# A vision tower on one core: the first group's batches in a new hand-written order, with sums in SBUF and the weights scaled on GpSimd

## The reference

```
h   = leaky(bn1(conv(x, stem_w, 4x4, stride 4)))        # 96 channels, 24 x 24
off = conv(h, off_w, 4x4, stride 4)                      # 32 channels, 6 x 6: a (y, x) offset for each of 16 taps
h   = leaky(bn2(deform_conv(h, off, dcn_w)))             # each tap samples h at a shifted point, from 4 corners
                                                         # 192 channels, 36 tokens an image
h   = h + attention(layernorm(h))                        # linear attention with random features, 12 heads
h   = h + experts(layernorm(h))                          # 3 experts of 192 x 768, top-1 gate per image
```

## Time and profile before

| what | value |
|---|---|
| median of 3 runs | 449.45 us (449.16 to 450.73) |
| the profiled execution's own time | 449.24 us |
| its span | 447.4 us |
| TensorE (PE) busy | 386.6 us, 86% |
| VectorE (DVE) busy | 287.8 us, 64% |
| ScalarE (ACT) busy | 223.4 us, 50% |
| GpSimd (POOL) busy | 163.0 us, 36% |
| chain that ended last | PE 65%, ACT 16%, DVE 13% |
| DMA | 54.18 MB, mean 121 GB/s |

### The profile page before, as it was taken

How to read it: one execution, slowest core, us unless ns; L and a number is a source line. 1 busy time by engine, 2 the same in 40 slices (tenths; PEclk the granted TensorE clock), 3 DMA queues, 4 the chain that set the end, 5 groups by cost and what they waited for, 6 DMA issues and landing times.

```text
span 447.4 us, 8176 instructions
## 1 busy us (share of the span) xinstructions
PE 386.6 (86%) x2856; PEld 279.6 (62%) x2856; DVE 287.8 (64%) x1108; ACT 223.4 (50%) x529; POOL 163.0 (36%) x168
## 2 busy tenths in 40 slices
PE   7986686878899797998988979788997979899997
PEld 3665254655678354876775768478575847767575
DVE  3842465745656677796666988765698876566222
ACT  2565545555536767544544475245448524542610
POOL 4116886700207676330067645107665300000000
PEclk9685567969699959999999999999999999999999
DMA  6578576843899953324855543104544200000000
GB/s 149 145 199 249 159 168 191 224 130 81 252 258 279 315 160 92 104 71 113 206 142 131 134 110 89 54 2 122 144 128 122 72 1 2 0 1 19 2 1 21
DMA packets 58480, 54.18 MB, mean 121 GB/s; under 512 B 42314, under 2 KB 50791, under 8 KB 58439
## 3 DMA queue, kind: packets, MB, share of 16 engines
q0 software_dynamic: 9216, 28.32, 22.5%
q1 hardware_dynamic: 48584, 25.28, 21.5%
q10 hardware_dynamic: 639, 0.05, 0.1%
HBM read 38.52 MB, written 15.11 MB: 120 GB/s over the span
## 4 chain that ended last, share of the span: by engine, by line
PE 65%; ACT 16%; DVE 13%; issue 4%; DMA 1%; SPq 1%; POOL 0%; ACTq 0%; DVEq 0%; POOLq 0%
PE bank L1065 10%; PE bank L1037 7%; PE bank L774 6%; PE bank L666 5%; PE bank L1044 5%; PE bank L689 4%; PE bank L703 4%; PE bank L971 4%; ACT bank L1248 3%; DVE bank L1557 2%; ACT hid L1400 2%; DVE o L1650 2%; PE bank L935 2%; PE bank L642 2%; DVE acc L1557 2%
## 5 line engine op out<-in xcount | busy, mean ns | idle before, releaser
L598 POOL DMA_INDIRECT ring<-cells,cell x144 | 150.0, 1041 | 167.3 <-DVE mv L1617 67.1
L1400 ACT ACTIVATE hid<-bank,b_up 128x288 f32<-128x288 f32 x72 | 32.0, 498 | 63.6 <-PE bank L1044 63.5
L1557 DVE SCALAR_TENSOR_TENSOR bank<-ring,corner,bank 128x96 f32<-128x96 f32 x224 | 52.9, 311 | 8.0 <-ACT bank L1248 7.9
L1065 PE MATMUL bank<-w_down,hid 128*128 128x192 f32 x288 | 52.1, 332 | 0.0
L1037 PE MATMUL bank<-xfT,w_up 128*128 128x288 f32 x144 | 44.8, 433 | 5.5 <-ACT hid L1400 5.3
L1065 PEld LDWEIGHTS bank<-w_down,hid 128*128 128x128 f32 x288 | 46.2, 190 | 4.6 <-issue 4.4
L774 PE MATMUL bank<-w_dcn,shared 128*128 128x192 f32 x192 | 42.6, 362 | 6.1 <-ACT shared L1257 6.1
L774 PEld LDWEIGHTS bank<-w_dcn,shared 128*128 128x128 f32 x192 | 33.6, 205 | 13.7 <-ACT shared L1257 9.8
L1037 PEld LDWEIGHTS bank<-xfT,w_up 128*128 128x128 f32 x144 | 25.0, 193 | 14.9 <-ACT hid L1400 7.8
L1505 DVE SCALAR_TENSOR_TENSOR h<-h 96x768 f32<-96x768 f32 x18 | 17.5, 994 | 25.1 <-ACT h L1236 23.7
L1248 ACT ACTIVATE bank<-ring,corner 128x96 f32<-128x96 f32 x112 | 31.4, 335 | 0.2 <-DMA ring<-cells,cell 0.2
(11 more groups left out here) (203 smaller groups left out, 648.0 us busy)
## 6 DMA issues: line engine op xcount, KB each, us to landing
cells<-ring SPq DMA_DIRECT2D x12, 864.0 KB, 8.7
xs<-in_x_dram SPq DMA_DIRECT2D x28, 108.0 KB
ring<-cells,cell POOLq DMA_INDIRECT x144, 3.1
cells<-w_up SPq DMA_DIRECT2D x2, 864.0 KB, 9.4
cells<-w_down SPq DMA_DIRECT2D x2, 864.0 KB, 7.5
w_down<-in_L_ffn_W_dram SPq DMA_DIRECT2D x3, 576.0 KB
hid<-in_L_tok_dcn_w_dram SPq DMA_DIRECT2D x1, 1152.0 KB, 7.6
w_up<-in_L_ffn_W_dram SPq DMA_DIRECT2D x3, 384.0 KB
```

Of the source, the lines that this page charges most:

```text
L598: pool.indirect_dma_start(ring[:, ring_slot(k), j, :], None, cells[g][0:HALF_CELLS, :] if k < EARLY else cells[g], bass.IndirectOffsetOnAx ...
L1065: mm = pe.matmul(down_out(e, t), hid[:, e % 2, f, t0:t0 + n], w_down[:, e, f, :], start=(f == 0), stop=(f == FCH - 1))
L1400: act.activation(hid[:, e % 2, f, :], up_bank(g, n)[:, 0:TOK], ACT.Gelu, bias=b_up[:, n:n + 1]).then_inc(gelu_done, 1)
L1557: ins = dve.scalar_tensor_tensor(acc[:, k % 3, :, j, :] if c == 3 else part_sum, ring[:, ring_slot(k), j, C1 * c:C1 * (c + 1)].rearrange(" ...
```

## The change

All of it lies in the front of the kernel, up to channels(0).

- **TensorE.** Ahead of the step only row units 0 to 5 of group 0 remain. Both offset halves of group 0 follow, then turn_unit(6), offsets_by_token(0) and product_unit(6), and only then row units 6 to 11, mixed with the transposes of the weights and the stem units 7 and 8. From there one written list of calls holds the nine batches, the stem units 9 to 17, the rows of group 1 (the first six ahead of dcn_turn(0, 0)), and row units 0 to 9 of group 2. Units 10 and 11 and group 2's offset halves stand behind fold_tokens(0). Row units alternate between two banks from group 1 on, and the weights use banks 0 to 2, so that the stem's transposes no longer wait for row copies.
- **ScalarE** and **VectorE** have such lists too. Row copies are shared out: VectorE takes the six odd ones of group 0, 1 to 6 of group 1 and 1 of group 2. It also takes three of the six copies of w_dcn. scale_dcn leaves ScalarE.
- **GpSimd** scales the weights, in 24 operations of 96 x 128, between rearrange_rows(1, 0) and rearrange_rows(1, 1).
- **Sums.** All of group 0's running sums are in SBUF, three deep: the first corner of batch k waits for the transpose of batch k - 3.
- **Homes.** Group 2's rows are copied into h, whose group 1 contents are done with by then, and no longer into the ring. So group 1's gathers don't wait for their store. The stem of group 3, which writes h, waits for that store instead of the offsets.
- **Loads.** Images (2,1) are loaded right behind (2,0). ld_ffn becomes ld_up and ld_down; up() waits for ld_up, the first down() and VectorE, at the step's end, for ld_down.

The diff's core (the written lists shortened):

```diff
-        def running(k):
-            if k < IN_SBUF:
+        def running(g, k):
+            if g == 0 or k < IN_SBUF:
...
-        FRONT_TURNS = {0: 9, 1: 10, 2: 11, 4: 12, 5: 13, 6: 14, 7: 15, 8: 16}
-        FRONT_ROWS = ((), (0,), (1, 2), (4, 5), (6,), (7, 8), (9,), (10, 11), ())
...
+        ROWS_ON_DVE = (range(1, 12, 2), (1, 2, 3, 4, 5, 6), (1,), ())
...
         def row_home(g, s):
+            if g == 2:
+                return h[:, s, :, :]
             return ht_first[s] if g == 1 else ht[:, s, :, :]
...
             load_images(2, 0)
+            load_images(2, 1)
             sp.wait_ge(gathered[ring_slot(2)], slot_done(0, 2))
...
+            def scale_dcn(i):
+                m, q = i // QUADS, i % QUADS
+                src = dcn_nat[:, m, :].rearrange("o (i c j q) -> o q i j c", i=CHUNKS, c=32, j=BATCH)[:, q, :, :, :]
+                for c in range(CHUNKS):
+                    ins = pool.tensor_scalar(dcn_perm[:, m, q, 128 * c:128 * c + 128].rearrange("o (j c) -> o j c", j=BATCH),
+                                             src[:, c], bn_scale[:, 1 + m:2 + m], None, ALU.mult)
+                ins.then_inc(dcn_scaled, 1)
 
...
-            for s in range(2):
-                rearrange_rows(1, s)
+            rearrange_rows(1, 0)
+            pool.wait_ge(ld_dcn, 16)
+            pool.wait_ge(bn_ready, 1)
+            for i in range(2 * QUADS):
+                scale_dcn(i)
+            rearrange_rows(1, 1)
...
+                offset_half(0, 0)
+                offset_half(0, 1)
                 turn_unit(6)
-                for n in (7, 8):
-                    turn_unit(n)
-                    product_unit(n - 1)
+                pe.wait_ge(ld_small, 16 * 6)
+                offsets_by_token(0)
+                product_unit(6)
+                row_unit(0, 6)
+                row_unit(0, 7)
+                row_unit(0, 8)
+                turn_unit(7)
+                row_unit(0, 9)
+                dcn_weights(0)
+                row_unit(0, 10)
+                dcn_weights(1)
+                row_unit(0, 11)
+                dcn_weights(2)
+                dcn_weights(3)
+                natural()
+                turn_unit(8)
...
+                row_unit(1, 5)
+                turn_unit(12)
+                dcn_turn(0, 0)
+                row_unit(1, 6)
+                row_unit(1, 7)
+                dcn_bias_rows()
...
+                dcn_products(0, 7)
+                row_unit(2, 7)
+                dcn_turn(0, 8)
+                row_unit(2, 8)
+                dcn_products(0, 8)
+                row_unit(2, 9)
                 fold_tokens(0)
-                product_unit(17)
+                row_unit(2, 10)
+                row_unit(2, 11)
+                offset_half(2, 0)
+                offset_half(2, 1)
...
+                if g == 1:
+                    stem_rows(3)
                 if g < 2:
-                    stem_rows(g + 2)
-                    pe.wait_ge(ht_even, 6 * (g + 3))
-                    pe.wait_ge(ht_odd, 6 * (g + 3))
+                    for done, count in last_rows(g + 2, 11):
+                        pe.wait_ge(done, count)
                 channels(g, xn, xn_ready, t2_mm, ROWTILES)
...
-                    pe.wait_ge(ld_ffn, 16 * 13)
+                    pe.wait_ge(ld_up, 16 * 9)
...
-                    act.wait_ge(off_mm, 2 * (g - 2) + (s + 1))
+                    act.wait_ge(h_stored[s], 32 * g)
...
-                if k >= IN_SBUF + 2:
+                if g == 0 and k >= 3:
+                    act.wait_ge(samp_mm, k - 2)
+                elif later(g) and k >= IN_SBUF + 2:
                     act.wait_ge(combined, BATCH * (BATCHES * g + k - 1))
-                elif k >= IN_SBUF:
...
+                dcn_weights(0)
+                row_copy(0, 10)
+                stem_turned(7)
+                dcn_weights(2)
+                stem_turned(8)
                 act.wait_ge(idx_ready, 2)
                 first_corners(0, 0)
-                for k in range(BATCHES):
-                    if k + 1 < BATCHES:
-                        first_corners(0, k + 1)
-                    if k in FRONT_SCALED:
-                        stem_scaled(FRONT_SCALED[k])
...
+                part_copy(0)
+                sample_points(0)
+                row_copy(0, 7)
+                row_copy(0, 9)
+                sample_corners(0)
+                row_copy(0, 11)
+                dcn_weights(1)
+                natural()
+                dcn_weights(3)
+                leaky(1, 0, 0, 1)
+                combine(0, 0, 1)
+                leaky(1, 0, 1, 2)
+                dcn_weights(5)
+                row_copy(1, 1)
...
+                combine(0, 7, 8)
+                leaky(2, 1, 1, 2)
+                combine(0, 8, 9)
+                dcn_tokens(0, range(FULL))
+                leaky(2, 1, 2, 3)
+                sample_corners(1)
+                dcn_tokens(0, (FULL,))
...
```

More of the change, by code:

```diff
@@ new lines, in dcn_first @@
+                turn_unit(14)
+                dcn_products(0, 1)
+                row_unit(1, 9)
+                row_unit(1, 10)
+                offsets_by_token(1)
+                dcn_turn(0, 3)
+                turn_unit(15)
+                row_unit(1, 11)
+                dcn_products(0, 2)
+                product_unit(14)
+                dcn_turn(0, 4)
+                turn_unit(16)
+                row_unit(2, 0)
+                row_unit(2, 1)
+                product_unit(15)
+                turn_unit(17)
@@ L1330, in combine_first @@
-                act.wait_ge(dcn_mm, BATCHES)
-                act.activation(xn[:, FULL, :], ps[2][:, 0:C2], ACT.Copy).then_inc(parts_evac, 1)
+                stem_scaled(7)
+                dcn_weights(4)
+                stem_turned(9)
+                stem_scaled(8)
+                row_copy(1, 0)
+                stem_turned(10)
+                stem_scaled(9)
+                first_corners(0, 1)
+                dcn_bias()
+                stem_scaled(10, 0, 1)
+                stem_turned(11)
@@ L1428, in _ @@
             stem_bn(0, 1)
[L1429 to L1438 removed]
+            for u in (0, 2, 4):
+                row_copy(0, u)
             def step(g, has_last, has_next):
```

372 lines of the change are left out of this document (222 added, 150 removed).

## The result

The changed kernel takes 443.1 us (median of 4 runs, 442.36 to 444.13) against 449.31 for the kernel before beside it (447.62 to 450.73): ratio 0.9865, 95% interval 0.9824 to 0.9905. It is faster, by 6.2 us (1.4%, with an interval that lies clear of 1), where 16.4 were forecast. The profiled execution has a span of 440.6 us.

What follows compares the result with a forecast made beforehand. Latency, with no engine full, was taken to bound the front from 19.75 to 125.39 us; channels(0) 16.4 earlier gave 449.24 - 16.4 = 432.8, or 433.0 against the median, range 427.5 to 443.

Steps and rivals of the forecast that it cites:

- GpSimd scales the weights: Ahead of the first gather: 24 scalings at 0.30 us, 7.2 in all, end at 27.5, before the gather's 33; cost 0.
- Rival 3: GpSimd's scaling is dear: at 0.667 us each the first gather starts at 37.7, time 436 us; chance 0.08.
- Offsets ahead of the second rows: Before the first gather: six row units move behind the offsets, gather 0 starts at 33.0 instead of 35.52, gain 2.5 us.
- travels alone: Store ahead of the gathers: the first half's cells go without the second half's, so gather 0's condition moves forward.
- Just hidden: Second half's cells: stored at 36.7, done 10 us later, in time for batch 3's gathers at 48.0.
- Gathers: Group 0's gathers: images (2,1) loaded earlier gain 1.8 us; last issue ends near 86.2, data lands at 91.3 (89 to 95).
- The batches: Group 0's nine batches: batch 2 summed at 63.7, six more at 5.35 us, with late items batch 8 at 99.
- late items: In the batches: items that come late hold their whole engine, 3 us added, bounds 0 and 11.
- rival 2: The fixed order stalls: 7.3 us a batch, batch 8 summed at 107.5, channels(0) at 117.5, time 441.4 us; chance 0.23.
- The tail: From batch 8's sum to channels(0): 10.0 us, so channels(0) starts at 109.0, 16.4 earlier.
- Checks at zero: The ld_ffn split, stem group 3's new wait and the next stage's lower DMA share: taken as 0 us gain or loss.
- rival 4: TensorE stays at 1.2 GHz from 35 to 125, busy 93 us, time 464 us, slower; chance 0.04.

Runs made afterwards that it cites:

- e1c: The changed kernel with the weights scaled on ScalarE again instead of GpSimd, third trial; 439.85 us (433.90 to 442.56), no ratio.
- e5b: The changed kernel with weights scaled on ScalarE and batch 0's first corner and sums taken up later; 433.20 us, 0.9602 of the kernel before.
- e1: The changed kernel with the weights scaled on ScalarE again, first trial, on a noisy chip; ratio 0.957 (0.948 to 0.967) to the kernel before.

## Why the prediction was wrong

channels(0) was forecast at 109.0 and came at 119.02. The miss of 10.0 by its own terms:

| term | forecast | measured | adds |
|---|---|---|---|
| first gather's start | 33.0 | 39.42 | 6.4 |
| from there to batch 0's sum | 12.0 | 13.75 (sum at 53.17) | 1.75 |
| to batch 2's sum | 18.7 | 17.65 (70.82) | -1.05 |
| to batch 8's sum | 35.3 | 37.7 (108.51) | 2.4 |
| to channels(0) | 10.0 | 10.5 | 0.5 |

**The step that failed is "GpSimd scales the weights".** The prediction took 0.30 us an operation, from a copy scaled by its elements, "Cost 0", with a cover that ends at 0.47. It measured 0.74 (17.70 / 24), inside the bounds of 0.15 and 1.36 but far above the value taken, and above even the whole copy of 4.5 times as many elements (0.667). A price by elements from another kind of operation was the wrong model: the runs show a strided scaling of 128 elements costing more than a copy of 576. Whether the 0.74 is a fixed part or goes by elements stays open, since no run changed the size of the operations or their number. The 6 us pause that the Trainium skill (GPSIMD Engine Reference, section 2.1, Instruction dispatch) states for a first call did not come: the 24 operations follow the copies within 0.1 us. Rival 3 had this mechanism, at a chance of 0.08 and 436 us; it erred by stopping at 0.667 and by letting the late start cost only its own length. The runs bear it out as the largest single cause: on the kernel before it costs 0.9%, and taken out of the changed kernel it brings channels(0) 4.1 of the 10.0 us forward, and 9.6 together with the early first corner, where that order alone brings nothing. In e1c, with the scaling gone and all else as in the change, 5.9 us of the miss are left: 2.7 at the first gather, 2.6 from there to batch 0's sum (14.6 for 12.0), -1.4 to batch 2's, 2.4 to batch 8's and -0.4 behind it.

e5b's 433.2 us and 109.38 are the forecast's 433.0 and 109.0, and that agreement is luck: e5b needed an order that the change doesn't have, its first gather came at 34.74 and not 33.0, batch 8's sum at 101.0 and not 99, and its tail took 8.4 and not 10.

**"Offsets ahead of the second rows"** was wrong by 1.7 to 2.7 us even so. The sampling index comes early (32.77 in e1c, forecast 32.3), but the gather also needs the first half's cells, and GpSimd waits for those:

```profile
35.68 1.11 POOL L608 DMA_INDIRECT ring<-cells,cell  x1 [7.59 <-DMA cells<-ring]
```

I had taken "travels alone" to mean sooner, but the first half's cells took at most 8.5 us from issue to landing in e1c and 8.9 before. Without the scaling the first gather starts at 34.7 to 35.7, as good as the old 35.52: the move of the offsets wins next to nothing.

**"Just hidden"** failed for the second half's store, issued at 41.58 and not 36.7: from the first gather to batch 3's first it takes 21.05 us (17.53 before, about 15 forecast). The twelve issues take 17.4 of them, 2.0 more than before, with the store under them, and GpSimd then stands 1.38 us ahead of the rearrangement of images (2,0), which SP issued only at 49.06, behind batch 0's landing. **"Gathers"** put the last issue's end at 86.2 and its data 5 us later; the end came at 99.5, the data 3.3 us behind it, and ScalarE took it at 104.15 without a wait. The landing was mis-sized further ahead: "landed 3.1 later" is the median of all 144 gathers, where those of batches 0 to 2 have a median of 6.0 in the changed kernel and the one that completes batch 0 took 5.63.

**"The batches"**: the first three had about the forecast pace, and the late items cost 5.4 us rather than 3, within the bounds of 0 and 11. That is 6.3 us a batch, half way to rival 2's 7.3; its 441.4 was near the result, but by waits for gathers and a late start, not by a stall of the order alone. **"The tail"** held, 10.5 for 10.0, and with it the gain from group 2's rows among the batches: the stage from the products to channels(0) fell from 16.27 to 5.92. **"Checks at zero"** held, 39.98 and 281.60 for "again about 40" and 282. The mean clock from 35 to 109 was 0.68, where above 0.8 was forecast, and rival 4's far slower case did not come either. One slip in the sums: the lower bound works out at 427.2, and the range began at 427.5; nothing hangs on it.

## What to carry to other kernels

Price an operation that an engine has not yet run by bounds, and follow the upper one through to what waits behind it: work moved to an idle engine isn't free when that engine holds the next stage's first issue. When an engine's order is written by hand, put work that needs no gather ahead of the wait for the gather, and don't expect it to pay until the late inputs are out of the way. At DMA shares of 0.83 to 0.98, as here, moving a transfer mostly moved a wait. And take a merged row of a queue apart before reading it as one long transfer: its length holds the waits between its issues.

## What was not expected of the hardware

- Beside GpSimd's TENSOR_SCALARs VectorE's small operations took two to three times as long: the CAST of 128x72 took 0.65 us in the changed kernel and 0.20 in e1c at the same place, and the nine operations of the index 4.81 us for 2.07. The Trainium skill (SBUF — State Buffer, "SBUF: two separate sides") says that GpSimd shares a port pair with VectorE's operations that have two SBUF inputs or run in a 2-port mode, as an exclusive lock, the other blocking for the whole instruction. The trace fits that: by it a 0.2 us operation beside a 0.74 us one can take up to 0.94, and 0.65 was seen, while the chain's first operation, which reads PSUM and SBUF, kept its 0.23. No run shows the modes. The prediction had allowed for such lengthening only from copies.
- On GpSimd a strided scaling of 128 columns took 0.74 us and a copy of 576 took 0.65, 5.8 and 1.1 ns a column. 48 memsets of 6 columns took 1.71 us together, 0.036 each and 5.9 ns a column. So the kind of operation counts between copy and scaling; between memset and scaling these numbers don't part kind from size.
- Chips differ. On two of them the kernel before took some 487 us for 449, and one kernel (e1) began channels(0) at 113.07 on the one and at 123.6 on the other, where TensorE was also held for up to 14.8 us with nothing to wait for. No profile of the other chips has such a hold.
